# Four attention layers on one core: the key loads of every batch but the first moved from SyncE's queue to GpSimd's, on semaphores of their own

## The chip, the cores and the metric

The kernel runs on one core of a Trainium2 chip. Its time is the device time of one execution in microseconds, and the time of a kernel is the median of its runs. TensorE (PE in the profile) multiplies matrices, VectorE (DVE), ScalarE (ACT) and GpSimd (POOL) work elementwise, and SyncE (SP) here issues DMA transfers only. All five work at once and wait for one another through semaphores; each takes its own instructions in order.

## The reference

Four cross-attention layers act one after the other on x of 4 batches x 1024 tokens x 256 channels, all in float32. Layers 0 and 2 ("wide") have 16 heads of 64 and 154 keys from a context of 512 channels, and a bias of two masks on some key columns. Layers 1 and 3 ("narrow") have RMS-normed queries, 16 query heads of 16 on 4 key heads, and attend to the same context..

```python
def wide(h, ctx, mask_A, mask_B, Wq, Wk, Wv, Wo, bo, idx_A, idx_B):   # layers 0 and 2
    q, k, v = heads(h @ Wq), heads(ctx @ Wk), heads(ctx @ Wv)
    logits = einsum("bhqd,bhkd->bhqk", q, k) * 64 ** -0.5 + col_bias  # -20 (1 - mask) on idx_A, idx_B
    return einsum("bhqk,bhkd->bhqd", softmax(logits), v) @ Wo + bo + h
def narrow(x, cond, wq, wk, wv, wo, norm_w):                          # layers 1 and 3
    q = heads(rmsnorm(x, norm_w) @ wq)
    k, v = kv_heads(cond @ wk), kv_heads(cond @ wv)
    return x + softmax(q @ k.T / 4) @ v @ wo
```

## The kernel before

It has three parts. `prepare` (to about 200 us) splits the weights into a high and a low float32 half and writes keys and values of all batches and layers to DRAM scratch. `run_layers` does the layers. `store_outputs` transposes x back and stores it.

`run_layers` works through eight windows w (or `it`), two pairs of layers times four batches (w // 4 is the pair, w % 4 the batch). A window has four chunks of four steps: chunks 0 and 2 are the two token halves of the wide layer, chunks 1 and 3 those of the narrow one; chunk 1 in window w finishes the batch of window w - 1. A step n has a query projection ("query"), maxima of the scores ("max") that are turned and taken off ("turn"), scores of the last 26 keys ("rest") and of the first 128 ("score"), and the product with the values ("value"). Behind a chunk come the sums ("sums", "inverse"), the scaling of the kept results ("scale", on GpSimd), their high and low half ("norm" on ScalarE, "low" on VectorE) and the output projection ("output"). Ahead of a narrow chunk stand "squares", "square" and "rate", the norm of x.

The order is written out by hand in ORDER (lines 517 to 561), a list of entries such as "max 11 4" (step 11, part 4); "0+" is step 0 of the next window, "3-" one of the window before. Every engine walks this one list and does what is its own in each entry, so an entry's place is its place in each engine's in-order stream. `each_batch` (line 743) walks it for the four computing engines; SyncE walks it in `one_round` (line 905), and only there do "early", "nkeys" and "wkeys" have a meaning.

The keys of a window lie in single buffers in SBUF. "wkeys" has four parts: `load_wide_keys` issues 4 DMAs (w_top) and then 5, 5 and 5 (w_pair, w_rest, w_aux; w_val, w_val_rest), line 812. "nkeys" has four parts of 14, 13, 13 and 13 DMAs in `load_narrow_keys`, line 844; most have 16 partitions. The first part of each waits until TensorE's last value step on the old keys has been done ("value 7 1" and "value 11 1"). At window 4, where the second pair of layers begins, `load_key_rows` adds 8 DMAs and a wait for them; other loads of new weights (lines 768, 793, 802) also stand in SyncE's stream.

The places that matter in ORDER, one after the other: "value 8 0, nkeys 0 0, scale 0 3, ..., inverse 1, norm 0 3, nkeys 0 1, squares 3, square 3, rate 3, nkeys 0 2, nkeys 0 3, query 12 0, scale 1 0, scale 1 1, split 0+, wkeys 0+ 0, wkeys 0+ 1, scale 2 0, max 0+ 0, scale 2 1, wkeys 0+ 2, wkeys 0+ 3, scale 2 2, scale 2 3", and "rest 0" of the next window.

GpSimd (lines 1132 to 1150) has four kinds of work: the low half of the query input in "split" and "rate" (x_lo, line 1137), the reciprocal root in "square" (a power, line 1142) and two products in each "scale" (line 1149), which wait for inv_b. SyncE brings inv_b from DRAM in `spread_inverses` (line 903), a new one after each "scale" and the first after "inverse" (line 935). ScalarE copies x to x_hi in "rate" (line 1033) and the scaled results to a_hi in "norm" (line 1088). TensorE waits for the narrow keys in "query 12" (line 1264), for w_top in "max 0" and for the other wide keys in "rest 0" (line 1306); its query products are line 1273, the rate transposes line 1396, the rest step line 1316 and the output line 1382.

Of the kernel before, what the change touches and what calls it, by code (L numbers as in the profile page):

```python
# [14 lines left out]
F32 = mybir.dt.float32  # L15
# [640 lines left out]
def run_layers(nc, ins, dr):  # L656

    ctx = ExitStack()
    with ctx:
# [60 lines left out]
        wtops_loaded, wkeys_loaded, nkeys_loaded = sem("wtops_loaded"), sem("wkeys_loaded"), sem("nkeys_loaded")  # L720
        early_loaded = signal("early_loaded", "split", times=16)
# [21 lines left out]
        def each_batch(eng, do):  # L743

            for r in ROUNDS:
                for what, n, k, turn in WINDOW:
                    if what not in ("early", "nkeys", "wkeys") and present(r + turn, what, n):
                        do(r + turn, what, n, k)
# [13 lines left out]

        @block.sync
        def _(sp):
# [3 lines left out]

            def load_key_rows(p):  # L770

                for par in range(2):
                    a = 64 * (1 - par)
                    def every(buf):
                        return buf[a:a + 6].rearrange("p (h two) k -> p h two k", two=2)[:, :, par, :]
                    rows = dr["keyrows"][p]
                    sp.dma_start(every(w_aux), rows[:, None, 0:P].to_broadcast([6, 8, P])).then_inc(key_rows_loaded, 16)
                    sp.dma_start(every(w_top), rows[:, None, :].to_broadcast([6, 8, KEYS])).then_inc(key_rows_loaded, 16)
                for j in range(4):
                    a = 64 * (1 - j % 2)  # L780
                    rests = w_aux_rest[a:a + 6].rearrange("p (g j) k -> p g j k", j=4)
                    sp.dma_start(rests[:, :, j, 0:REST],
                                 dr["keyrows"][p][:, None, P:KEYS].to_broadcast([6, 4, REST])).then_inc(key_rows_loaded, 16)
# [19 lines left out]

            def cols(src, b):

                return src[..., bass.ds(b * P, P)], src[..., bass.ds(b * REST + B * P, REST)]

            def load_wide_keys(p, b, part):

                def go(dst, src, loaded=wkeys_loaded):
                    sp.dma_start(dst, src).then_inc(loaded, 16)

                def every(buf, par):
                    return buf.rearrange("p (h two) k -> p h two k", two=2)[:, :, par, :]

                if part == 0:
                    for par in range(2):
                        rows = slice(64 * par, 64 * par + 64)
                        main, rest = cols(dr["wk_hib"][p, rows], b)  # L820
                        go(every(w_top[rows], par)[:, :, 0:P], main, wtops_loaded)
                        go(every(w_top[rows], par)[:, :, P:KEYS], rest, wtops_loaded)
                elif part < 3:
                    par = part - 1
                    rows = slice(64 * par, 64 * par + 64)
                    main, _ = cols(dr["wk_hi"][p, rows], b)
                    rest = dr["wk_rest"][p, rows][..., bass.ds(b * REST, REST)]
                    for half in range(2):
                        to = slice(64 * half, 64 * half + 64)
                        go(every(w_pair[to], par).bitcast(F32), main)  # L830
                        go(every(w_rest[to], par)[:, :, 0:REST], rest)
                    main, _ = cols(dr["wk_lob"][p, rows], b)
                    go(every(w_aux[rows], par), main)
                else:
                    go(w_val[:], dr["wv"][p, bass.ds(b, 1)].rearrange("o p n -> p (o n)"))
                    for j in range(4):
                        dst = w_val_rest[32 * j:32 * j + REST].rearrange("p (g d) -> p g d", d=DW)
                        src = dr["wv_rest"][p, bass.ds(b * REST, REST)].rearrange("p (g j d) -> p g j d", j=4, d=DW)
                        go(dst, src[:, :, j, :])

            def load_narrow_keys(p, b, j):

                def go(dst, src):
                    sp.dma_start(dst, src).then_inc(nkeys_loaded, 16)

                def by_unit(src, w):
                    return src.rearrange("(u i) k -> i u k", i=DN)

                heads = lambda buf: buf.rearrange("p (u j) k -> p u j k", j=4)[:, :, j, :]
                main, rest = cols(dr["nk_hi"][p], b)  # L850
                for half in range(2):
                    to = slice(64 * half + DN * j, 64 * half + DN * j + DN)
                    go(heads(n_pair[to]).bitcast(F32), by_unit(main, P))
                    go(n_pair_rest[to, :, 32 * j:32 * j + REST].bitcast(F32), by_unit(rest, REST))
                lo, lo_rest = cols(dr["nk_lob"][p], b)
                hi, hi_rest = cols(dr["nk_hib"][p], b)
                for par in range(2):
                    to = slice(64 * par + DN * j, 64 * par + DN * j + DN)
                    odd = lambda ap: ap.rearrange("p (v two) k -> p v two k", two=2)[:, :, par, :]
                    go(odd(heads(n_aux[to])), odd(by_unit(lo, P)))  # L860
                    go(odd(n_aux_rest[to, :, 32 * j:32 * j + REST]), odd(by_unit(lo_rest, REST)))
                    go(odd(heads(n_top[to]))[:, :, 0:P], odd(by_unit(hi, P)))
                    go(odd(heads(n_top[to]))[:, :, P:KEYS], odd(by_unit(hi_rest, REST)))
                go(n_val_rest[32 * j:32 * j + REST], dr["nv_rest"][p, bass.ds(b * REST, REST)])
                if j == 0:
                    go(n_val[:], dr["nv"][p, bass.ds(b, 1)].rearrange("o p g d -> p (o g) d"))
# [38 lines left out]
            def one_round(r):  # L905

                for what, c, k, turn in WINDOW:
# [46 lines left out]
                    elif (what, c, k) == ("output", 2, 3) and w == B - 1:  # L954

                        wait(sp, pe_output.sem, pe_output.after(w, what, c, k))
                        wait(sp, dve_output.sem, dve_output.after(w, what, c, k))
                        load_wide_out(1)
                    elif (what, c, k) == ("query", 11, 1) and w == B - 1:

                        wait(sp, pe_query.sem, pe_query.after(w, what, c, k))
                        load_wide_query(1)
                    elif what == "early" and (w, c) != (0, 0):

                        before_w, before = back_chunk(w, c)
                        key = ("split" if before % 2 == 0 else "rate", before, 0)
                        wait(sp, act_split.sem, act_split.after(before_w, *key))
                        wait(sp, pool_split.sem, pool_split.after(before_w, *key))
                        if (w, c) == (B, 0):
                            sp.wait_ge(wide_query_loaded, 2 * WIDE_QUERY)  # L970
                        load_early(HALF[c], b)
                    elif what == "nkeys" and w > 0:

                        if k == 0:
                            wait(sp, pe_value.sem, pe_value.after(w, "value", 7, 1))
                            if w == B:
                                load_narrow_query(1)
                        if k == KVN - 1 and w == B:
                            sp.wait_ge(narrow_query_loaded, 2 * NARROW_QUERY)
                        load_narrow_keys(p, b, k)  # L980
                    elif what == "wkeys" and w > 0:

                        if k == 0:
                            wait(sp, pe_value.sem, pe_value.after(w - 1, "value", 11, 1))
                            if w == B:
                                load_key_rows(1)
                                sp.wait_ge(key_rows_loaded, 2 * KEY_ROWS)
                        load_wide_keys(p, b, k)
# [5 lines left out]
            load_wide_keys(0, 0, 0)  # L994
            load_key_rows(0)
            sp.wait_ge(cleared, CLEARED)
            for part in range(1, 4):
                load_wide_keys(0, 0, part)
# [5 lines left out]
            for part in range(KVN):  # L1004
                load_narrow_keys(0, 0, part)
# [89 lines left out]
        def _(pool):  # L1095
# [37 lines left out]
            def do(it, what, n, k):  # L1133
# [9 lines left out]
                elif what == "scale":  # L1143
# [6 lines left out]
                    last.then_inc(pool_scale.sem, 1)  # L1150

# [89 lines left out]
        def _(pe):  # L1241
# [19 lines left out]
            def do(it, what, n, k):  # L1261
                if what == "query":
                    if n == 3 * 4:
                        wait(pe, nkeys_loaded, (it + 1) * NKEYS)
# [10 lines left out]
                elif what == "max":  # L1275
                    if k == 0 or k == 4 and wide(n):
                        wait(pe, dve_aux.sem, dve_aux.after(it, *query_for(n, k // 4)))
                        if n == 0:
                            wait(pe, wtops_loaded, (it + 1) * WTOPS)
# [21 lines left out]
                elif what in ("rest", "score"):  # L1301
# [3 lines left out]
                    if (what, n) == ("rest", 0):  # L1305
                        wait(pe, wkeys_loaded, (it + 1) * WKEYS)
# [191 lines left out]
```

## Time and profile before

| | us |
|---|---|
| median of 3 runs | 1894.06 |
| lowest and highest | 1888.15, 1894.6 |
| the profiled execution | 1887.3 |
| its span, first to last instruction | 1885.2 |

| engine | busy us | share of the span | instructions |
|---|---|---|---|
| TensorE | 1707.6 | 91% | 10924 |
| VectorE | 1250.4 | 66% | 2393 |
| ScalarE | 1039.0 | 55% | 1761 |
| GpSimd | 428.5 | 23% | 299 |

A profile is of one execution and 2.1 us shorter in span than the execution's own time. A busy time is a sum over the instructions of an engine; a DMA issue counts for none, so SyncE has no row.
### The profile page before, as it was taken

The page shows a single profiled execution, that of the slowest core. Times are in us where ns is not written, and L with a number is a line of the kernel's source. Part 1 is how long each engine was busy: PE and PEld are TensorE (multiplying, and loading weights), DVE is VectorE, ACT ScalarE, POOL GpSimd, SP SyncE. Part 2 cuts the span into 40 slices and gives each one's busy share as a digit, 9 for nine tenths or more (in the row PEclk, how much of TensorE's full clock was granted, in tenths as well). Part 3 has the DMA queues.
Part 4 walks back from the last instruction along what each step waited for, and adds up shares of the span by engine and source line. Part 5 has one row for each costly group of instructions (what it writes and reads, how often), then busy time and mean ns, then how long its engine had stood idle before and what let it go on. Part 6 is the DMA issues. An engine that isn't in the chain of part 4 may idle for free. (4 is left out here: it accounts for less than half of the span.)

```text
span 1885.2 us, 29948 instructions
## 1 busy us (share of the span) xinstructions
PE 1707.6 (91%) x10924; PEld 938.6 (50%) x10924; DVE 1250.4 (66%) x2393; ACT 1039.0 (55%) x1761; POOL 428.5 (23%) x299
## 2 busy tenths in 40 slices
PE   6897596989999999999899999899999999999564
PEld 5786343444545454545445454445454545454333
DVE  4447554667867686778567777577777777776432
ACT  1111063666666666666556666566666666666231
POOL 4242302121212121212111312131313121312201
PEclk9998688999999999999999999899999999999786
DMA  7986541051216131612242324222322333222105
GB/s 272 310 274 213 128 127 47 13 101 35 75 44 124 35 73 46 124 36 74 89 95 86 82 52 99 57 71 59 83 65 71 60 82 66 70 60 60 47 25 200
DMA packets 173272, 175.78 MB, mean 93 GB/s; under 512 B 89345, under 2 KB 129661, under 8 KB 171016
## 3 DMA queue, kind: packets, MB, share of 16 engines
q1 hardware_dynamic: 170824, 163.39, 33.1%
q10 hardware_dynamic: 2304, 10.49, 1.4%
q8 instruction: 88, 1.44, 0.3%
q14 instruction: 56, 0.46, 0.1%
HBM read 127.17 MB, written 46.63 MB: 92 GB/s over the span
## 5 line engine op out<-in xcount | busy, mean ns | idle before, releaser
L1189 DVE TENSOR_REDUCE tops<-general 128x2 bf16<-128x308 f32 x1024 | 436.5, 472 | 107.1 <-PE general L1292 48.6
L1149 POOL TENSOR_TENSOR kept<-kept,inv_b 128x512 f32<-128x512 f32 x192 | 258.5, 1367 | 650.5 <-DMA inv_b<-scratch_inverses 650.5
L1052 ACT ACTIVATE probs<-score_ps 128x512 f32<-128x512 f32 x512 | 299.1, 597 | 139.1 <-PE score_ps L1328 131.9
L1176 DVE CAST q_aux<-q_pair 64x512 bf16<-64x512 f32 x160 | 78.1, 488 | 208.2 <-ACT q_pair L1040 207.4
L1062 ACT ACTIVATE q_aux<-general 4x512 bf16<-4x512 bf16 x320 | 187.3, 585 | 13.7 <-PE general L1299 6.9
L1039 ACT ACTIVATE q_pair<-general 64x512 fp32r<-64x512 f32 x160 | 94.5, 591 | 178.4 <-PE general L1273 178.2
L1088 ACT ACTIVATE a_hi<-kept 128x512 fp32r<-128x512 f32 x192 | 109.9, 621 | 121.9 <-PE general L1382 66.5
L1202 DVE TENSOR_TENSOR a_lo<-kept,a_hi 128x512 fp32r<-128x512 f32 x192 | 157.0, 858 | 28.6 <-ACT a_hi L1088 27.5
L1222 DVE TENSOR_TENSOR x<-general,x 128x512 f32<-128x512 f32 x160 | 108.6, 690 | 80.8 <-PE general L1382 79.5
L1288 PE MATMUL general<-w_top,q_aux 128*128 128x154 bf16 x1024 | 125.9, 234 | 23.9 <-DVE q_pair L1179 10.8
L1137 POOL TENSOR_TENSOR x_lo<-xn,x_hi 128x1024 fp32r<-128x1024 f32 x32 | 75.8, 2368 | 311.9 <-ACT x_hi L1020 161.0
L1343 PE MATMUL out_ps<-probs,w_val 128*64 128x512 f32 x512 | 137.0, 619 | 0.7 <-ACT probs L1052 0.7
L1074 ACT ACTIVATE kept<-out_ps 128x512 f32<-128x512 f32 x192 | 104.2, 595 | 57.3 <-PE sum_ps L1357 42.2
L1292 PE MATMUL general<-n_top,q_aux 128*128 128x308 bf16 x512 | 129.3, 300 | 6.5 <-DVE q_aux L1177 2.8
L1327 PE MATMUL score_ps<-q_pair,n_pair 128*128 128x512 f32 x256 | 125.1, 497 | 8.8 <-ACT probs L1052 7.3
L1273 PE MATMUL general<-x_hi,wq_hi 128*128 128x512 f32 x256 | 115.5, 451 | 19.0 <-POOL x_lo L1137 18.6
L1288 PEld LDWEIGHTS general<-w_top,q_aux 128*128 128x128 bf16 x1024 | 79.3, 99 | 102.6 <-issue 37.5
L1382 PE MATMUL general<-a_hi,wo_hi 128*128 128x512 f32 x256 | 113.2, 442 | 13.7 <-DVE q_pair L1179 5.9
L1327 PE MATMUL score_ps<-q_pair,w_pair 128*128 128x512 f32 x256 | 122.2, 482 | 0.8
L1178 DVE TENSOR_TENSOR q_pair<-general,q_pair 64x512 fp32r<-64x512 f32 x160 | 109.5, 684 | 5.0
L1179 DVE TENSOR_TENSOR q_pair<-general,q_pair 64x512 fp32r<-64x512 f32 x160 | 111.0, 693 | 2.2
L1052 ACT ACTIVATE probs_rest<-score_ps 128x512 f32<-128x512 f32 x128 | 76.2, 595 | 54.9 <-PE score_ps L1328 38.1
(150 smaller groups left out, 3252.0 us busy)
## 6 DMA issues: line engine op xcount, KB each, us to landing
inv_b<-scratch_inverses SPq DMA_DIRECT2D x128, 256.0 KB
inv_b<-scratch_inverses SPq DMA_DIRECT2D x128, 128.0 KB
xn<-scratch_stream SPq DMA_DIRECT2D x16, 512.0 KB, 4.1
w_pair<-scratch_wk_hi SPq DMA_DIRECT2D x32, 256.0 KB
x<-scratch_stream SPq DMA_DIRECT2D x16, 512.0 KB, 3.4
scratch_stream<-x SPq DMA_DIRECT2D x16, 512.0 KB, 3.9
scratch_wk_hi<-p_kout_hi SPq DMA_DIRECT2D x16, 308.0 KB
p_raw<-in_L_xattn_Wk_dram SPq DMA_DIRECT2D x4, 1024.0 KB, 8.2
```

The lines of the kernel that those rows point to most:

```text
L1052: nc.scalar.activation(dst, score_ps[:, number % 2, :], ACT.Exp, scale=scale).then_inc(act_exp.sem, 1)
L1062: last = nc.scalar.activation(q_aux[a:a + 4, half_of(n), slot(n), j, :], ps[0:4].bitcast(BF16)[:, 0:TOK], ACT.Copy, scale=-1.0)
L1149: last = nc.gpsimd.tensor_tensor(tile, tile, inv_b[:, i, :], ALU.mult)
L1179: last = nc.vector.tensor_tensor(q_pair[0:64, s, j + 1, :], ps[64:P], q_pair[64:P, s, j + 1, :], ALU.subtract)
L1189: last = nc.vector.tensor_reduce(tops[:, n % 2, sub, 2 * pair:2 * pair + 2], src, AX_X, ALU.max)
L1202: last = nc.vector.tensor_tensor(a_lo[:, i, :], kept[:, place(tile), :], a_hi[:, i, :], ALU.subtract)
L1273: last = nc.tensor.matmul(ps, l, r, start=(i == 0), stop=(i == len(pairs) - 1))
L1288: last = nc.tensor.matmul(ps[:, i * KEYS:(i + 1) * KEYS], q[:, 2 * pair + i, sub], w_top[:, 4 * (n % 4) + 2 * pair + i, :], start=True, st ...
L1292: last = nc.tensor.matmul(ps[:, 0:2 * KEYS], q[:, n % 2, sub], n_top[:, h:h + 2, :].rearrange("p h k -> p (h k)"), start=True, stop=True)
L1327: nc.tensor.matmul(ps, keys[0], q_pair[:, s, unit, :], start=True, stop=False)
L1343: last = nc.tensor.matmul(out_ps[64 * i:64 * i + 64, k, :], w_val[:, h * DW:(h + 1) * DW], probs[:, 2 * k + i, :], start=True, stop=False, ...
L1382: last = nc.tensor.matmul(ps, l, r, start=(i == 0), stop=(i == len(pairs) - 1))
```

## The change

SyncE keeps the keys of window 0. Those of windows 1 to 7, narrow and wide, and the key rows of the second pair are issued by GpSimd, at the same entries of ORDER. The three loading functions move out of SyncE's block to the scope around it and take the engine and the semaphore as arguments; what they move is unchanged. Four new semaphores count GpSimd's loads, and TensorE waits on them from window 1 on. `each_batch` now passes "nkeys" and "wkeys" on; the other computing engines have no branch for them. The two waits on "value" go along to GpSimd, and SyncE keeps the one ahead of its narrow query weights at window 4.

```diff
@@ semaphores @@
+        wtops_again, wkeys_again, nkeys_again = sem("wtops_again"), sem("wkeys_again"), sem("nkeys_again")
+        key_rows_again = sem("key_rows_again")
@@ each_batch @@
-                    if what not in ("early", "nkeys", "wkeys") and present(r + turn, what, n):
+                    if what != "early" and present(r + turn, what, n):
@@ the loads, now outside SyncE's block @@
+        def load_key_rows(eng, p, loaded):
...
+        def load_wide_keys(eng, p, b, part, loaded, tops):
+            def go(dst, src, loaded=loaded):
+                eng.dma_start(dst, src).then_inc(loaded, 16)
...
+        def load_narrow_keys(eng, p, b, j, loaded):
+            def go(dst, src):
+                eng.dma_start(dst, src).then_inc(loaded, 16)
...
@@ SyncE, one_round @@
-                        if k == 0:
+                        if k == 0 and w == B:
                             wait(sp, pe_value.sem, pe_value.after(w, "value", 7, 1))
-                            if w == B:
-                                load_narrow_query(1)
+                            load_narrow_query(1)
                         if k == KVN - 1 and w == B:
                             sp.wait_ge(narrow_query_loaded, 2 * NARROW_QUERY)
-                        load_narrow_keys(p, b, k)
-                    elif what == "wkeys" and w > 0:
-
-                        if k == 0:
-                            wait(sp, pe_value.sem, pe_value.after(w - 1, "value", 11, 1))
-                            if w == B:
-                                load_key_rows(1)
-                                sp.wait_ge(key_rows_loaded, 2 * KEY_ROWS)
-                        load_wide_keys(p, b, k)
@@ GpSimd @@
+                elif what == "nkeys" and it > 0:
+
+                    if k == 0:
+                        wait(pool, pe_value.sem, pe_value.after(it, "value", 7, 1))
+                    load_narrow_keys(pool, it // B, it % B, k, nkeys_again)
+                elif what == "wkeys" and it > 0:
+
+                    if k == 0:
+                        wait(pool, pe_value.sem, pe_value.after(it - 1, "value", 11, 1))
+                        if it == B:
+                            load_key_rows(pool, 1, key_rows_again)
+                            pool.wait_ge(key_rows_again, KEY_ROWS)
+                    load_wide_keys(pool, it // B, it % B, k, wkeys_again, wtops_again)
@@ TensorE @@
-                        wait(pe, nkeys_loaded, (it + 1) * NKEYS)
+                        wait(pe, nkeys_loaded if it == 0 else nkeys_again, max(it, 1) * NKEYS)
...
-                            wait(pe, wtops_loaded, (it + 1) * WTOPS)
+                            wait(pe, wtops_loaded if it == 0 else wtops_again, max(it, 1) * WTOPS)
...
-                        wait(pe, wkeys_loaded, (it + 1) * WKEYS)
+                        wait(pe, wkeys_loaded if it == 0 else wkeys_again, max(it, 1) * WKEYS)
```

## Rows read from the trace of the kernel before

**Rows 1.** The page, first part: TensorE's busy time, share of the span, instructions.

```profile
PE 1707.6 (91%) x10924; PEld 938.6 (50%) x10924; DVE 1250.4 (66%) x2393; ACT 1039.0 (55%) x1761; POOL 428.5 (23%) x299
```

**Rows 2.** Windows from query 12 to query 12: length, busy time by engine, clock, DMA.

```profile
549.00:738.00 189.00, 185.66 (x1249) 95.91 (x1248) 141.03 (x267) 125.24 (x217) 43.20 (x31) 1.00 0.30 70
738.00:932.00 194.00, 186.25 (x1250) 95.91 (x1250) 141.63 (x267) 126.59 (x218) 46.68 (x33) 1.00 0.32 78
932.00:1127.00 195.00, 189.92 (x1247) 98.21 (x1248) 139.45 (x266) 124.39 (x215) 40.50 (x28) 0.97 0.32 81
1127.00:1324.00 197.00, 187.00 (x1249) 96.26 (x1248) 139.95 (x267) 125.08 (x216) 43.47 (x31) 0.97 0.31 69
```

**Rows 3.** Waits of TensorE, 300 to 1760 us: who for whom, total us, times, longest.

```profile
PE score_ps L1316 <- issue: 9.7, 2, 9.0
PE score_ps L1327 <- ACT probs L1052: 7.1, 4, 3.9
...
PE general L1273 <- DMA n_val_rest<-scratch_nv_rest: 5.8, 1, 5.8
```

**Rows 4.** Timeline of SyncE's queue: start us, us, engine line op, [idle before]; narrow keys.

```profile
509.57 0.34 SPq L844 DMA_DIRECT2D n_pair<-scratch_nk_hi  x1
...
539.66 0.43 SPq L844 DMA_DIRECT2D n_pair_rest<-scratch_nk_hi  x1
540.13 0.43 SPq L844 DMA_DIRECT2D n_pair<-scratch_nk_hi  x1
...
930.43 0.40 SPq L844 DMA_DIRECT2D n_val_rest<-scratch_nv_rest  x1
```

**Rows 5.** Timeline of GpSimd, windows 1 and the turn to 2.

```profile
546.88 2.36 POOL L1137 TENSOR_TENSOR x_lo<-xn,x_hi 128x1024 fp32r<-128x1024 f32 x1 [8.65 <-ACT x_hi L1033]
549.21 2.52 POOL L1149 TENSOR_TENSOR kept<-kept,inv_b 128x512 f32<-128x512 f32 x2
...
581.92 2.59 POOL L1149 TENSOR_TENSOR kept<-kept,inv_b 128x512 f32<-128x512 f32 x2 [14.50 <-DMA inv_b<-scratch_inverses]
590.26 2.51 POOL L1149 TENSOR_TENSOR kept<-kept,inv_b 128x512 f32<-128x512 f32 x2 [5.74 <-DMA inv_b<-scratch_inverses]
```

**Rows 6.** Timeline of TensorE: rate transposes, query 12, first rest step, query 12 of window 3.

```profile
543.24 0.65 PE L1396 MATMUL general<-ident,rate 128*128 128x128 f32 x4
...
549.35 0.47 PE L1273 MATMUL general<-x_hi,nq_hi 128*128 128x512 f32 x1
...
608.48 1.06 PE L1316 MATMUL score_ps<-q_pair,w_rest 128*32 128x512 f32 x8 [0.74 <-issue]
...
932.18 0.80 PE L1273 MATMUL general<-x_hi,nq_hi 128*128 128x512 f32 x1 [5.77 <-DMA n_val_rest<-scratch_nv_rest]
```

**Rows 7.** GpSimd's groups of instructions, shapes apart: operation, shapes, count, busy us, mean ns.

```profile
L1142 POOL TENSOR_TENSOR rate<-meansq,power 128x4 f32<-128x4 f32 x16 | 16.1, 1009 | 308.2 <-DVE meansq L1226 308.2
...
L1117 POOL TENSOR_SCALAR_AFFINE_SELECT w_aux<-w_aux 4x512 bf16<-4x512 bf16 x4 | 2.5, 632 | 0.6 <-POOL x_lo L1137 0.2
...
L1488 POOL MEMSET const-float32-0.0<- 128x1 f32 x1 | 0.1, 99 | 0.2 <-issue 0.2
```

**Rows 8.** Windows of 2 us behind TensorE's longest wait, columns as in rows 2.

```profile
1192.00:1194.00 2.00, 1.16 (x8) 0.44 (x12) 1.49 (x3) 0.00 (x0) 0.00 (x0) 0.50 0.73 160
1194.00:1196.00 2.00, 2.00 (x11) 0.56 (x3) 0.00 (x0) 0.60 (x1) 0.00 (x0) 0.50 0.61 119
1196.00:1198.00 2.00, 2.00 (x9) 1.60 (x9) 0.08 (x1) 0.60 (x1) 1.99 (x2) 0.92 0.07 16
```

**Rows 9.** Timeline of ScalarE: the copies that read "scale 0 3" and "scale 2 2".

```profile
525.79 1.15 ACT L1088 ACTIVATE a_hi<-kept 128x512 fp32r<-128x512 f32 x2 [1.73 <-PE general L1382]
...
606.23 1.15 ACT L1088 ACTIVATE a_hi<-kept 128x512 fp32r<-128x512 f32 x2 [2.37 <-PE general L1382]
```

**Rows 10.** Timeline of SyncE's queue: one wide key load.

```profile
577.58 0.63 SPq L812 DMA_DIRECT2D w_rest<-scratch_wk_rest  x1
```

**Rows 11.** VectorE's casts into q_aux, whole run: duration ns min/median/max, first and last start.

```profile
L1176 DVE CAST q_aux<-q_pair x160: 408/420/1547, 223.0 to 1795.9; 64x512 bf16<-64x512 f32 x160
```

More of the change, by code:

```diff
@@ L761, in bank_of, with every @@
             return general[:, BANK[use], :]
+        def load_key_rows(eng, p, loaded):
+            for par in range(2):
+                a = 64 * (1 - par)
+                def every(buf):
+                    return buf[a:a + 6].rearrange("p (h two) k -> p h two k", two=2)[:, :, par, :]
+                rows = dr["keyrows"][p]
+                eng.dma_start(every(w_aux), rows[:, None, 0:P].to_broadcast([6, 8, P])).then_inc(loaded, 16)
+                eng.dma_start(every(w_top), rows[:, None, :].to_broadcast([6, 8, KEYS])).then_inc(loaded, 16)
+            for j in range(4):
+                a = 64 * (1 - j % 2)
+                rests = w_aux_rest[a:a + 6].rearrange("p (g j) k -> p g j k", j=4)
+                eng.dma_start(rests[:, :, j, 0:REST],
+                             dr["keyrows"][p][:, None, P:KEYS].to_broadcast([6, 4, REST])).then_inc(loaded, 16)
@@ new lines, in cols, with every @@
+        def cols(src, b):
+            return src[..., bass.ds(b * P, P)], src[..., bass.ds(b * REST + B * P, REST)]
+        def load_wide_keys(eng, p, b, part, loaded, tops):
+            def go(dst, src, loaded=loaded):
+                eng.dma_start(dst, src).then_inc(loaded, 16)
+            def every(buf, par):
+                return buf.rearrange("p (h two) k -> p h two k", two=2)[:, :, par, :]
+            if part == 0:
+                for par in range(2):
+                    rows = slice(64 * par, 64 * par + 64)
+                    main, rest = cols(dr["wk_hib"][p, rows], b)
+                    go(every(w_top[rows], par)[:, :, 0:P], main, tops)
+                    go(every(w_top[rows], par)[:, :, P:KEYS], rest, tops)
+            elif part < 3:
+                par = part - 1
+                rows = slice(64 * par, 64 * par + 64)
+                main, _ = cols(dr["wk_hi"][p, rows], b)
+                rest = dr["wk_rest"][p, rows][..., bass.ds(b * REST, REST)]
+                for half in range(2):
+                    to = slice(64 * half, 64 * half + 64)
+                    go(every(w_pair[to], par).bitcast(F32), main)
+                    go(every(w_rest[to], par)[:, :, 0:REST], rest)
+                main, _ = cols(dr["wk_lob"][p, rows], b)
+                go(every(w_aux[rows], par), main)
+            else:
+                go(w_val[:], dr["wv"][p, bass.ds(b, 1)].rearrange("o p n -> p (o n)"))
+                for j in range(4):
+                    dst = w_val_rest[32 * j:32 * j + REST].rearrange("p (g d) -> p g d", d=DW)
+                    src = dr["wv_rest"][p, bass.ds(b * REST, REST)].rearrange("p (g j d) -> p g j d", j=4, d=DW)
+                    go(dst, src[:, :, j, :])
@@ new lines, in load_narrow_keys, with by_unit @@
+        def load_narrow_keys(eng, p, b, j, loaded):
+            def go(dst, src):
+                eng.dma_start(dst, src).then_inc(loaded, 16)
+            def by_unit(src, w):
+                return src.rearrange("(u i) k -> i u k", i=DN)
+            heads = lambda buf: buf.rearrange("p (u j) k -> p u j k", j=4)[:, :, j, :]
+            main, rest = cols(dr["nk_hi"][p], b)
+            for half in range(2):
+                to = slice(64 * half + DN * j, 64 * half + DN * j + DN)
+                go(heads(n_pair[to]).bitcast(F32), by_unit(main, P))
+                go(n_pair_rest[to, :, 32 * j:32 * j + REST].bitcast(F32), by_unit(rest, REST))
+            lo, lo_rest = cols(dr["nk_lob"][p], b)
+            hi, hi_rest = cols(dr["nk_hib"][p], b)
+            for par in range(2):
+                to = slice(64 * par + DN * j, 64 * par + DN * j + DN)
+                odd = lambda ap: ap.rearrange("p (v two) k -> p v two k", two=2)[:, :, par, :]
+                go(odd(heads(n_aux[to])), odd(by_unit(lo, P)))
+                go(odd(n_aux_rest[to, :, 32 * j:32 * j + REST]), odd(by_unit(lo_rest, REST)))
+                go(odd(heads(n_top[to]))[:, :, 0:P], odd(by_unit(hi, P)))
+                go(odd(heads(n_top[to]))[:, :, P:KEYS], odd(by_unit(hi_rest, REST)))
+            go(n_val_rest[32 * j:32 * j + REST], dr["nv_rest"][p, bass.ds(b * REST, REST)])
+            if j == 0:
+                go(n_val[:], dr["nv"][p, bass.ds(b, 1)].rearrange("o p g d -> p (o g) d"))
@@ L768, in load_wide_query @@
                     sp.dma_start(wq[i][:].bitcast(F32), dr["wq_" + a][p]).then_inc(wide_query_loaded, 16)
[L770 to L783, printed above, removed]
             def load_wide_out(p):
@@ L802, in load_narrow_out @@
                             sp.dma_start(dst[:, :, v, :].bitcast(F32), src[v, j]).then_inc(narrow_out_loaded, 16)
[L804 to L866, printed above, removed]
@@ L993, in _ @@
             load_masks()
[L994 to L995 removed]
+            load_wide_keys(sp, 0, 0, 0, wkeys_loaded, wtops_loaded)
+            load_key_rows(sp, 0, key_rows_loaded)
             sp.wait_ge(cleared, CLEARED)
             for part in range(1, 4):
[L998 removed]
+                load_wide_keys(sp, 0, 0, part, wkeys_loaded, wtops_loaded)
             load_wide_out(0)
@@ L1004, in _ @@
             for part in range(KVN):
-                load_narrow_keys(0, 0, part)
+                load_narrow_keys(sp, 0, 0, part, nkeys_loaded)
             sp.wait_ge(wide_out_loaded, WIDE_OUT)
```

## The prediction

> **What bounds the kernel now.** The page comes first: TensorE is busy 91% of the span, and in its second part TensorE's line is nines and a few eights from the ninth slice to the last three, so the layers are bound by TensorE and everything else works in its shadow [rows 1]. The windows cut at the start of the third narrow query (query 12) come next: an undisturbed stage of one batch takes 189 us (the first row stands for three such), three take 194, 195 and 197 [rows 2]. So the time that the layers lose beyond their own rhythm is 5 + 6 + 8 = 19 us in all. The list of what TensorE waited for between 300 and 1760 us gives two causes that have to do with keys: 5.8 us for the last narrow key load, once, and 9.7 us ahead of the first rest step, nearly all of it one wait of 9.0 us [rows 3]. Those two waits are the most that a faster supply of keys could take away, and the reader should hold on to that: a change of who issues the keys has little to win.
>
> What it can lose is read from SyncE's own timeline. SyncE issues a narrow key load every 0.47 us (539.66, 540.13), and in window 1 it starts as early as 509.57 [rows 4]. GpSimd's timeline of the same stretch shows the work among which the loads are to stand [rows 5], and TensorE's the two moments that matter: the rate transposes at 543.24 and query 12 at 549.35, with no idle time noted for either [rows 6].
>
> **The change, part by part.** SyncE loses 72 issues per batch: 53 narrow (14 + 13 + 13 + 13) and 19 wide (4 + 5 + 5 + 5). The same 72 go into GpSimd's in-order stream, at the places that ORDER gives them, for seven batches. The two waits per batch on TensorE's value steps, the eight key-row loads and a wait for their landing go along. TensorE's own waits change their semaphore, not their number; I cost that at nothing, as each waits for the same data. No byte more is moved.
>
> Let t be GpSimd's time for one narrow issue. No row of this trace shows a DMA issued by GpSimd, so t is bounded. From below: SyncE's pitch of 0.47 us [rows 4]; GpSimd's cheapest operation, a fill of one column, takes 0.10 us, but that one writes nothing but a constant [rows 7]. From above: 1.6 us, the power operation (1.01 us) and the small diagonal fill (0.63 us) one after the other [rows 7]. I take t = 1.0 us. The nearest row is the power operation on four columns: it has next to no data, so its 1.01 us is a routine's fixed cost, and a DMA issue is again a routine with next to no data of its own. The rest is worked out at 1.0, and repeated at the ends.
>
> *Narrow keys, parts 2 and 3 (26 loads).* Here is the step that decides. In ORDER they stand behind "rate 3" and ahead of "query 12". On SyncE that was harmless, since SyncE does nothing in "rate". On GpSimd "rate 3" is the subtraction x_lo, which waits 8.65 us for ScalarE and ends at 546.88 + 2.36 = 549.24 [rows 5]. Query 12 starts at 549.35, 0.1 us later [rows 6], and the same pair of times, 0.1 us apart, recurs in all other windows but the one with the wait. So the 26 loads can't begin before the very moment at which TensorE wants them landed. The landing takes 1.75 us from the last issue: SyncE's last load of window 3 starts at 930.43, TensorE goes on at 932.18 [rows 4, 6]. The new wait is 26 x 1.0 + 1.75 - 0.10 = 27.65 us per batch. Nothing hides it: TensorE is in order, and value 10, the rest step and the maxima of chunk 3 stand behind query 12. Behind the loads on GpSimd stands "scale 1 0", which began at once at 549.21 and now runs 26 us later, that is beside the same wait, so it adds nothing; the next late thing after the wait is TensorE alone.
>
> *What a wait costs beyond itself.* After the 9.0 us wait the granted clock shows 0.50 in 1192 to 1196 and 0.92 in the next 2 us: that is 1.2 of 2.4 GHz for 1.16 + 2.00 us of matmul work, and a little of 2 us more [rows 8]. Lost: (1.16 + 2.00) / 2 + 0.16 = 1.7 us. A wait of 28 us lets the clock fall all the same. So 27.65 + 1.7 = 29.4 us, times seven: 205.5 us.
>
> *Narrow keys, parts 0 and 1 (27 loads).* They may start at 509.5, when the value step that frees the buffers has ended (SyncE's first one started at 509.57 [rows 4]). 14 loads end at 523.5, "scale 0 3" (2.5 us) at 526.0; ScalarE starts the copy that reads it at 525.79 [rows 9], so 0.2 us late. 13 more loads end at 539.0, the power operation at 540.0; TensorE's rate transposes start at 543.24 [rows 6]. Cost nothing at t = 1.0, with TensorE's 3.2 us of slack as cover. The cover is gone at 27 t + 2.5 + 1.0 = 33.7, so t = 1.12; beyond that each 0.1 us costs 2.7 us per batch (4.9 us at t = 1.3, 13 us at 1.6).
>
> *Wide keys.* A wide issue keeps SyncE for 0.63 us, a narrow one for 0.43, with 0.04 between two [rows 4, 10]: a factor 0.67 / 0.47 = 1.4, which I carry over: 1.4 us each. Parts 0 and 1, nine loads, 12.6 us, lie in the 14.5 us in which GpSimd waits ahead of 581.92 [rows 5]: hidden. Parts 2 and 3, ten loads, begin when "scale 2 1" ends at 592.8 and end at 606.8 in place of a free 7.2 us; "scale 2 2" then ends at 609.3, and ScalarE wants it at 606.23 [rows 5, 9]: 3.1 us late. ScalarE is in order too, and the exponentials of the next scores stand behind that copy, so I count all of it: times seven, 21.5 us. The keys themselves land at about 608.5, when the rest step wants them at 608.48 [rows 6].
>
> *Once, at window 4.* Eight key-row loads and their landing, 8 x 1.0 + 1.75, come ahead of the nine wide ones: 22.4 us against 14.5. 7.9 us late, where 3.9 us of waiting already lies in that stage of 195 us [rows 2, 3]: plus 4 us.
>
> *What is won.* In window 3 the keys stood behind two loads of query weights, and the 5.8 us with its low clock (1.7 us) is part of the new wait now: 7.5 us. In window 4 the 16 loads of narrow output weights no longer hold up the last wide keys, but they still hold up inv_b, which goes out behind them: I count 1.5 us of the 9.0. The 36 us per batch that SyncE no longer spends on issues buy no more, since inv_b is on time in the 189 us stages.
>
> The Trainium skill speaks against the move in two places. "SBUF — State Buffer", Who interferes with whom, says that VectorE in a two-port mode and GpSimd block each other for a whole instruction, and that descriptors of a GpSimd DMA wait for it. The trace agrees that something holds them up: VectorE's casts take 0.42 us and up to 1.55 [rows 11]. Four pairs of casts lie between 509 and 540, 3.4 us, just above the slack of 3.2; by that the sum would be 7 x 0.2 = 1.4 us more, and nothing in the stretch of 26 loads, where VectorE has run dry. "DMA: Bandwidth & Descriptors", Latency and other measured facts, puts the first byte of a DMA from GpSimd at about 1 us against 0.6; by that the landing would be 0.4 us later, 2.8 us in all. No run here shows it.
>
> **Sum.** 205.5 + 21.5 + 4 - 7.5 - 1.5 = 222 us on top of the profiled execution's 1887.3 us, which is 2109 us. That execution is 6.8 us under the median of the runs, 1894.06, and about equal to the fastest; put on the median, 2116, and I say 2115 us.
>
> **The rivals.**
> *Cheap issues (0.22).* GpSimd issues at SyncE's pace, t = 0.47, wide ones at 0.65. Then the wait is 12.2 + 1.65 = 13.9 us, with the clock 15.6, times seven 109; all else is hidden, window 4 gets its 3.9 us back too, and 13 us are won: about 1990 us. For it speaks that the loads are small (16 partitions); against it that SyncE's issues are done by a queue that does nothing else. At t = 0.7 it is 2035.
> *Dear issues (0.22).* t = 1.3, wide ones 1.8: the wait is 35.5 us, with the clock 37.2; narrow parts 0 and 1 add 4.9, the wide ones 7.1; times seven 344; with the rest (10 more at window 4, 9 won) 2240 us. At 1.6 us it is 2385. For it speaks that the wide loads have 512 rows each, and that something must write these down; against it that SyncE's price rises by 1.4 only.
> *Faster than before (0.03).* GpSimd hands its DMAs over without being held up, a tenth of a microsecond each as for its cheapest operation, and the 19 us of the disturbed stages come back. But even so 26 x 0.1 + 1.65 = 4.3 us per batch is waited, 30 us in all. The sign turns where the wait is under 19 / 7 = 2.7 us, so at t = 0.04 us, or where the loads run ahead of x_lo. It would then be about 1870 us. Against it stands the order: the wait for ScalarE stands in the same stream ahead of them.
> *No effect (0.03).* GpSimd's stream isn't in order for DMAs and the loads land in time as before: 1890 us.
>
> **How the numbers follow.** My forecast, t from 0.85 to 1.15, has 0.50: 2070 to 2165 us. The likeliest time is its middle. For eight times in ten the range takes in most of the cheap and of the dear case: 2015 (t = 0.6) to 2250 us (t a little over 1.3). A measurement of this kernel can tell 0.5%, some 9 us. Slower by more than that: 0.50 + 0.22 + 0.22 = 0.94, and 0.01 of what is left; faster 0.02; the same 0.03.
>
> **What would show it.** In the profile after, seven waits of TensorE at query 12, for a DMA that fills narrow keys, of some 28 us each; stages of about 220 us; GpSimd's 26 issues back to back from the end of x_lo; no 5.8 us apart in window 3. If these waits are there with another length, t was wrong and nothing else. If x_lo or the power operation comes late, parts 0 and 1 are dearer than I think. The prediction is wrong in kind if the loads start before x_lo has ended, or if TensorE's waits stand at the scales and not at the query.

## The result

| | before | after |
|---|---|---|
| median, us | 1892.6 | 1994.22 |
| lowest and highest | 1888.15, 1894.6 | 1993.7, 1995.69 |
| the profiled execution | 1887.3 | 1993.7 |
| its span | 1885.2 | 1991.6 |

The kernel before has one run more here than when the forecast was made. The change makes the kernel slower: the ratio is 1.0545, 95% interval 1.0526 to 1.0564. By the two medians that is 101.6 us, by the two profiled executions 106.4 us. The forecast was 2115 us, with a range from 2015 to 2250 us: the kernel is slower, as forecast, but by 102 us and not by some 220.

The page of the kernel after, its first line and the two queues that carry the work (packets, MB, share of 16 engines' time):

```profile
PE 1721.1 (86%) x10924; PEld 943.9 (47%) x10924; DVE 1248.5 (63%) x2393; ACT 1038.5 (52%) x1761; POOL 710.4 (36%) x811
...
q1 hardware_dynamic: 92648, 141.87, 25.2%
q0 software_dynamic: 18960, 21.53, 6.0%
```

TensorE has the same 10924 instructions in a longer span; that they take 1721.1 us in place of 1707.6 [rows 1] is put down to slow clock further down (e2). A queue that was not there before, q0, has taken over 21.5 MB. GpSimd's busy time is 710.4 us against 428.5: unlike an issue of SyncE, a DMA issue of GpSimd does count as busy, so what is said of issues beside the table of the kernel before holds for SyncE alone.

The windows of the kernel after, cut at query 12, with columns as in [rows 2]:

```profile
567.00:771.00 204.00, 187.46 (x1248) 96.88 (x1248) 139.19 (x266) 125.36 (x216) 82.69 (x103) 0.97 0.27 64
771.00:976.00 205.00, 187.79 (x1248) 96.89 (x1248) 140.48 (x266) 125.35 (x216) 83.72 (x103) 0.97 0.30 74
976.00:1181.00 205.00, 188.11 (x1248) 96.70 (x1248) 143.89 (x266) 125.47 (x216) 89.27 (x111) 0.97 0.31 77
1181.00:1389.00 208.00, 190.34 (x1248) 98.58 (x1248) 139.85 (x266) 125.12 (x216) 77.79 (x95) 0.96 0.28 65
```

Each stage takes 204 to 208 us where an undisturbed one took 189. The busy times of all engines but GpSimd are those of before within about 2%. What TensorE waited for between 300 and 1860 us (total, times, longest):

```profile
PE general L1278 <- DMA n_val_rest<-scratch_nv_rest: 99.2, 7, 14.4
...
PE general L1387 <- DVE a_lo L1207: 4.8, 2, 4.6
PE score_ps L1332 <- ACT probs L1044: 4.8, 4, 4.3
...
PE score_ps L1321 <- issue: 3.9, 3, 1.8
```

The first line is nearly the whole result. It stands for seven waits, 99.2 us in all and 14.2 on average, where before there was one of 5.8 us [rows 3]. The line of the rest step, 9.7 us with one wait of 9.0 there, is down to 3.9 us. GpSimd's timeline of window 1:

```profile
513.64 0.59 POOL L821 DMA_DIRECT2D n_pair<-scratch_nk_hi  x1 [3.13 <-PE out_ps L1374]
...
520.88 3.03 POOL L1141 TENSOR_TENSOR kept<-kept,inv_b 128x512 f32<-128x512 f32 x2
...
541.05 1.03 POOL L1134 TENSOR_TENSOR rate<-meansq,power 128x4 f32<-128x4 f32 x1 [10.61 <-DVE meansq L1231]
550.70 2.37 POOL L1129 TENSOR_TENSOR x_lo<-xn,x_hi 128x1024 fp32r<-128x1024 f32 x1 [8.62 <-ACT x_hi L1025]
553.01 0.56 POOL L821 DMA_DIRECT2D n_pair<-scratch_nk_hi  x1
...
565.57 0.53 POOL L821 DMA_DIRECT2D n_val_rest<-scratch_nv_rest  x1
566.11 2.50 POOL L1141 TENSOR_TENSOR kept<-kept,inv_b 128x512 f32<-128x512 f32 x2
...
613.54 0.71 POOL L789 DMA_DIRECT2D w_pair<-scratch_wk_hi  x1
```

and TensorE's:

```profile
547.06 0.65 PE L1401 MATMUL general<-ident,rate 128*128 128x128 f32 x4
...
567.45 0.79 PE L1278 MATMUL general<-x_hi,nq_hi 128*128 128x512 f32 x1 [14.14 <-DMA n_val_rest<-scratch_nv_rest]
```

x_lo ends at 550.70 + 2.37 = 553.07. The first of the 26 issues starts at 553.01 and the last at 565.57, and "scale 1 0" comes behind them. TensorE goes on at 567.45, after 14.14 us of waiting. The length of an issue is in GpSimd's groups, shapes apart (count, busy us, mean ns):

```profile
L821 POOL DMA_DIRECT2D n_aux_rest<-scratch_nk_lob x56 | 28.5, 508 | 0.0
...
L789 POOL DMA_DIRECT2D w_rest<-scratch_wk_rest x28 | 19.1, 682 | 0.0
...
L789 POOL DMA_DIRECT2D w_val<-scratch_wv x7 | 4.1, 582 | 0.0
```

A narrow issue takes 0.508 us, a wide one with 512 rows 0.682, and w_val's, with few long rows, 0.582.

### The profile page after: what moved, and what is told of

The parts are those of the page before. It is cut to its first block and busy times, and to the rows that moved or that the text cites. A ratio compares the mean times of both kernels' runs of the same rounds, so it can differ in the third digit from the quotient of the medians.

```text
span 1991.6 us, 29949 instructions
## 1 busy us (share of the span) xinstructions
PE 1721.1 (86%) x10924; PEld 943.9 (47%) x10924; DVE 1248.5 (63%) x2393; ACT 1038.5 (52%) x1761; POOL 710.4 (36%) x811
## 3 DMA queue, kind: packets, MB, share of 16 engines
q1 hardware_dynamic: 92648, 141.87, 25.2%
q0 software_dynamic: 18960, 21.53, 6.0%
## 5 line engine op out<-in xcount | busy, mean ns | idle before, releaser
L1278 PE MATMUL general<-x_hi,nq_hi 128*128 128x512 f32 x64 | 33.2, 519 | 104.1 <-DMA n_val_rest<-scratch_nv_rest 99.2
```

The lines of the kernel that those rows point to most:

```text
L1278: last = nc.tensor.matmul(ps, l, r, start=(i == 0), stop=(i == len(pairs) - 1))
```

## The experiments

Two theories were open after the comparison. By the first, the loss is made by the place of the narrow parts 2 and 3 in GpSimd's stream, behind x_lo, and by nothing else. By the second, loads from GpSimd are dearer wherever they stand. Four smaller questions were open too: what a wait costs beyond its length, whether the wide loads cost anything, what VectorE does to GpSimd's issues, and where a gain is to be had.

**The two parts ahead of x_lo (e1).** The kernel after, with two entries of ORDER moved:

```diff
-        max 10 3, score 9 3, max 10 4, value 9 0, max 10 5, max 10 6, square 3, max 10 7, query 11 0,
+        max 10 3, score 9 3, max 10 4, value 9 0, max 10 5, nkeys 0 2, max 10 6, square 3, max 10 7, nkeys 0 3, query 11 0,
         query 11 1, turn 10, value 9 1, rate 3, max 11 0, max 11 1,
-    rest 10, max 11 2, score 10 0, max 11 3, nkeys 0 2, max 11 4, max 11 5, score 10 1, nkeys 0 3,
+    rest 10, max 11 2, score 10 0, max 11 3, max 11 4, max 11 5, score 10 1,
```

> The changed kernel with two entries of ORDER moved: narrow part 2 stands ahead of 'square 3', part 3 ahead of 'rate 3', so all 53 narrow issues on GpSimd are over before x_lo. Theory (the place in GpSimd's stream decides): the seven waits of 14.2 us at query 12 go, with about 1.7 us of low clock each: 1994 - 7 x 15.9 = 1883 us, a few us under the kernel before. Rival (loads from GpSimd are costly wherever they stand: slow landings, late scales): the waits shrink but 20 us or more of the loss stay, 1912 us or above.

Measured: 1880.12 us, ratio to before 0.9938 (0.992 to 0.9956). GpSimd's timeline in window 1, and under it TensorE's query 12:

```profile
534.61 0.53 POOL L821 DMA_DIRECT2D n_val_rest<-scratch_nv_rest  x1
539.21 1.03 POOL L1134 TENSOR_TENSOR rate<-meansq,power 128x4 f32<-128x4 f32 x1 [4.06 <-DVE meansq L1231]
...
546.27 0.54 POOL L821 DMA_DIRECT2D n_val_rest<-scratch_nv_rest  x1
548.96 2.36 POOL L1129 TENSOR_TENSOR x_lo<-xn,x_hi 128x1024 fp32r<-128x1024 f32 x1 [2.15 <-ACT x_hi L1025]
551.28 2.52 POOL L1141 TENSOR_TENSOR kept<-kept,inv_b 128x512 f32<-128x512 f32 x2
```

```profile
551.42 0.47 PE L1278 MATMUL general<-x_hi,nq_hi 128*128 128x512 f32 x1
```

Part 2 ends at 535.1, ahead of the power operation; part 3 lies between 540.20 and 546.81, in time that GpSimd otherwise spends waiting for x_hi; 2.15 us of that wait are left. x_lo ends at 551.32 and query 12 starts at 551.42 with no idle time. All seven waits at query 12 are gone, and the time is under that of the kernel before, with the same 72 loads on the same engine. So the second theory falls as the cause of the loss; a small price of the wide loads comes out below (e3).

**The same move with all keys on SyncE (e5).** The kernel before, with the same edit of ORDER.

> The kernel before, all keys on SyncE, with the same two entries moved. Theory: only the 5.8 us wait of window 3 goes, because the narrow keys now stand ahead of the wide query weights in SyncE's queue; with its low clock 7 us, so 1885 us; the 9.0 us wait of window 4 stays. Rival (the order has no part, the gain of the other kernel is GpSimd's): 1892 us. If the order alone does as well as the order with GpSimd, GpSimd brings nothing.

Measured: 1879.67 us, ratio 0.9939 (0.9917 to 0.996). TensorE's waits there:

```profile
PE score_ps L1316 <- issue: 8.9, 1, 8.9
...
PE score_ps L1327 <- ACT probs L1052: 6.6, 6, 3.1
```

The wait of 5.8 us in window 3 is gone. The one of 8.9 us stays; it stands at the first rest step of window 5, behind the loads of window 4. SyncE alone with the order does as well as GpSimd with the order. I had expected 1885 us, 7 us less than before; the interval is 7.6 to 15.7 us, and what makes up the rest is not shown.

**Wide keys alone on GpSimd (e3).** Narrow keys go back to SyncE:

```diff
+                        load_narrow_keys(sp, p, b, k, nkeys_loaded)
...
-                    if what != "early" and present(r + turn, what, n):
+                    if what not in ("early", "nkeys") and present(r + turn, what, n):
...
-                        wait(pe, nkeys_loaded if it == 0 else nkeys_again, max(it, 1) * NKEYS)
+                        wait(pe, nkeys_loaded, (it + 1) * NKEYS)
```

> Wide keys and key rows on GpSimd, narrow keys back on SyncE. Theory: no wait at query 12 but the one of window 3 (5.8 us); 19 issues of 0.7 us lie in GpSimd's idle time, window 4's wait of 9.0 us shrinks to about 5: 1885 to 1892 us. Rival (wide issues make the scales late): 3 us and more per batch, 1912 us or above.

Measured: 1889.38 us, ratio 0.9994 (0.9979 to 1.0009). GpSimd's timeline around the wide loads of window 1:

```profile
575.87 0.68 POOL L789 DMA_DIRECT2D w_aux<-scratch_wk_lob  x1
586.67 2.53 POOL L1143 TENSOR_TENSOR kept<-kept,inv_b 128x512 f32<-128x512 f32 x2 [10.12 <-DMA inv_b<-scratch_inverses]
...
601.93 2.38 POOL L789 DMA_DIRECT2D w_val_rest<-scratch_wv_rest  x4
605.08 2.97 POOL L1143 TENSOR_TENSOR kept<-kept,inv_b 128x512 f32<-128x512 f32 x2 [0.76 <-DMA inv_b<-scratch_inverses]
```

Nine of them end at 576.55, 10 us ahead of "scale 2 0". The other ten end at 604.3, and "scale 2 2" starts at 605.08, still with 0.76 us of idle time for inv_b. It is the same in all seven windows: both scales that stand behind wide loads wait for inv_b. So the wide loads hold up no scale, and in sum they cost nothing that can be measured. Of the 9.0 us at the first rest step of window 5, 1.6 are left, with 4.8 us for a_lo behind them.

They are not free, though. SyncE writes the sums of a chunk to DRAM and reads them back (scratch_sums, spread_sums), and VectorE's reciprocal waits for them. On SyncE the first four wide loads (w_top) stood behind that round trip; on GpSimd they go out as soon as x_lo has ended, beside it. The kernel before:

```profile
567.77 0.53 SPq L916 DMA_DIRECT2D scratch_sums<-wide_sums  x1
569.63 0.34 SPq L925 DMA_DIRECT2D spread_sums<-scratch_sums  x1
570.02 2.58 SPq L812 DMA_DIRECT2D w_top<-scratch_wk_hib  x4
571.49 0.55 DVE L1196 RECIPROCAL inv<-spread_sums 128x64 f32<-128x64 f32 x1
```

and e3:

```profile
570.36 2.83 POOL L789 DMA_DIRECT2D w_top<-scratch_wk_hib  x4
570.77 0.53 SPq L918 DMA_DIRECT2D scratch_sums<-wide_sums  x1
573.65 0.34 SPq L927 DMA_DIRECT2D spread_sums<-scratch_sums  x1
578.86 0.55 DVE L1203 RECIPROCAL inv<-spread_sums 128x64 f32<-128x64 f32 x1 [4.50 <-DMA spread_sums<-scratch_sums]
```

From the first issue to the reciprocal it takes 8.1 us, where it took at most 3.7 before. Six windows of e3 have such a wait of VectorE, of 3.0 to 4.5 us, and so have e1 and the kernel after (1.4 to 4.5 us); in before, e4, e5 and e8, with the wide keys on SyncE, none at that place is longer than 0.3 us. TensorE pays for part of it: from query 12 of window 0 to query 4 of window 1 it needs 97.3 to 97.8 us in the six kernels with wide keys on GpSimd, and 93.0 to 95.7 in the four others. So about 2 us are lost there, 1 to 5 us in the next window (99.2 us in e1, 99.4 in e3 and 96.8 in e7, against 95.6 before and 94.7 in e5), and none that can be seen in later ones. That eats up most of the 6.5 us that the wide keys bring at windows 4 and 5 (below). e3 beside e4 shows that the wide loads on GpSimd do it; that it is the moment of w_top, and what its data and the sums share, is not shown, as no run moves w_top alone.

**Narrow keys alone on GpSimd (e4).** This is the mirror image: wide keys and key rows go back to SyncE.

> Narrow keys on GpSimd, wide ones back on SyncE. Theory: the seven waits of 14.2 us stay, and the 9.0 us wait of window 4 comes back in part: 1994 to 2000 us. Rival (the loss is shared by the wide loads): clearly under 1990 us.

Measured: 2001.28 us, ratio 1.0583 (1.0557 to 1.0609).

```profile
PE general L1285 <- DMA n_val_rest<-scratch_nv_rest: 102.2, 7, 17.4
PE score_ps L1328 <- issue: 8.4, 2, 7.8
```

The time is 1.3 us above the range expected. The seven waits carry all of the loss. One of them is 17.4 us long, with a gap of 3.05 us between GpSimd's issues for which the trace names no cause, and the wait at the first rest step of window 5 is back (7.8 us).

**Half of the issues behind x_lo (e2).** As e1, but part 3 stays where it was, at "rest 10":

> The changed kernel with narrow part 2 moved ahead of 'square 3' and part 3 left where it was, so 13 issues in place of 26 lie between x_lo and query 12. If a wait is (issues x 0.505) + 1.65 us of landing, it is now 8.2 us, seven times. If the low clock behind a wait costs 1.7 us whatever the wait's length: 1880 + 7 x (8.2 + 1.7) = 1949 us. If what a wait costs beyond itself grows with its length (half as much here): 1943 us. If a fixed price per wait outweighs the issues (a landing of 5 us or more): above 1965 us.

Measured: 1947.68 us, ratio 1.0318 (1.0294 to 1.0341).

```profile
PE general L1278 <- DMA n_val_rest<-scratch_nv_rest: 53.5, 7, 7.7
```

These are seven waits of 7.6 us. 13 issues fewer save 45.7 us of waiting in all, so 6.5 per wait and 0.50 us per issue, which is the length of an issue; a line through the two points leaves 1.1 us that doesn't depend on the number.

Against e1 the time is 67.6 us longer and the waits are 53.5, so each costs 2.0 us beyond its length; for the kernel after, 114.1 and 99.2, it is 2.1. The three were not timed together; with the ratios to the kernel before of each comparison the two numbers are 2.6 and 2.2. TensorE's busy time gives the same without any such comparison: e1 has 1704.8 us, e2 1721.9 and the kernel after 1721.1, for the same instructions, so 2.4 and 2.3 us more per wait. It is a price per wait, and not one that grows with the microseconds waited. Most of it is seen in the windows around the wait of window 1 of the kernel after (TensorE's busy time first, the granted clock third from the end):

```profile
554.00:566.00 12.00, 0.00 (x0) 0.00 (x0) 0.00 (x0) 0.00 (x0) 12.00 (x25) 0.64 0.18 21
566.00:568.00 2.00, 0.55 (x1) 0.50 (x2) 0.00 (x0) 0.00 (x0) 1.98 (x3) 0.50 0.05 8
568.00:570.00 2.00, 2.00 (x6) 1.32 (x4) 0.00 (x0) 0.00 (x0) 0.61 (x1) 0.50 0.09 29
570.00:572.00 2.00, 2.00 (x11) 0.83 (x12) 0.36 (x1) 1.55 (x3) 0.00 (x0) 0.76 0.71 191
572.00:574.00 2.00, 2.00 (x24) 0.36 (x32) 1.86 (x4) 1.97 (x4) 0.51 (x1) 1.00 0.91 238
```

The clock has gone to 1.2 of 2.4 GHz during the wait; it stays there for 2.55 us of work and for half of the next 2 us: 0.55 / 2 + 2.00 / 2 + 0.24 x 2.00 = 1.75 us. The same sum behind the wait of 7.7 us in e2 (0.50 in 561 to 563, 0.67 in 563 to 565) gives 1.6. Where the other half microsecond goes is not shown.

**Copies on VectorE beside the 26 issues (e6).** The kernel after, and in VectorE's part of query 12, ahead of its wait:

```diff
+                    if n == 12 and it > 0:
+                        for i in range(36):
+                            made = 36 * (it - 1) + i
+                            wait(dve, copied, made - 2)
+                            nc.vector.tensor_copy(idle_out[:, made % 3], idle_in[:]).then_inc(copied, 1)
```

> The changed kernel plus 36 VectorE copies of a constant tile (float32, 128 x 512) ahead of VectorE's part in query 12 of windows 1 to 7, that is beside GpSimd's 26 issues, while VectorE has nothing else to do. If copies and GpSimd's descriptor writing shut each other out, the 26 issues stretch from 13.1 us to 20 us or more and the time is 1994 + 7 x 7 = 2043 us or above. If they don't meet, an issue keeps its 0.505 us, the copies end inside the wait, and the time is 1994 to 2000 us.

Measured: 2014.47 us, ratio 1.067 (1.0648 to 1.0692). GpSimd's issues, VectorE's copies in the same stretch, and TensorE's waits:

```profile
553.15 0.68 POOL L823 DMA_DIRECT2D n_aux<-scratch_nk_lob  x1
...
561.21 0.68 POOL L823 DMA_DIRECT2D n_pair_rest<-scratch_nk_hi  x1
...
562.54 0.51 POOL L823 DMA_DIRECT2D n_aux_rest<-scratch_nk_lob  x1
...
564.53 0.50 POOL L823 DMA_DIRECT2D n_aux_rest<-scratch_nk_lob  x1
```

```profile
550.22 12.23 DVE L1185 COPY idle_out<-idle_in 128x512 f32<-128x512 f32 x36
```

```profile
PE general L1286 <- DMA n_val_rest<-scratch_nv_rest: 120.5, 7, 17.3
```

While the copies run, to 562.45, an issue takes 0.67 or 0.68 us (the first 0.78); from 562.54 on it is 0.51 again. 36 copies in 12.23 us are 0.34 each, so an issue takes the time of just two copies, and each ends 0.1 us behind the end of a copy. The copies keep their pace. The seven waits are 17.2 us on average, against 14.2. That is 21.3 us in all, and the time grew by 20.2 (24 by the ratios). The trace agrees with the rule of the Trainium skill that the prediction weighed ("SBUF — State Buffer", Who interferes with whom), in that GpSimd is held until an instruction of VectorE has ended. But neither of the two expectations has the size: with copies as short as these the issue is held up by 0.17 us, and is not shut out for the whole run of 36.

**The output weights later (e7 and e8).** At window 4 SyncE loads 16 pieces of narrow output weights ahead of the last inv_b. e7 is e1 and e8 is e5, both with those loads behind it:

```diff
                         wait(sp, pool_scale.sem, pool_scale.after(w, what, c, k))
                         spread_inverses(c, k + 1)
+                        if (w, c, k) == (B, 2, 2):
+                            wait(sp, pe_output.sem, pe_output.after(w, "output", 1, 1))
+                            load_narrow_out(1)
                     elif (what, c, k) == ("output", 1, 1):
...
-                        if w == B:
-                            wait(sp, pe_output.sem, pe_output.after(w, what, c, k))
-                            load_narrow_out(1)
```

> e1 (keys on GpSimd, narrow parts 2 and 3 ahead of x_lo) and, once, at window 4, SyncE's 16 loads of narrow output weights moved from ahead of the last inv_b loads of chunk 2 to behind them. Theory: the 4.6 us wait for a_lo that e1 still has there goes, with its low clock: 1880 - 6 = 1874 us. Rival (the wait comes from elsewhere, or turns up behind the later loads): 1880 us.

> The reordered kernel with all keys on SyncE (e5) and the same move of the 16 output weight loads. Theory: the 8.9 us wait at the first rest step of window 5 goes, since the last wide keys no longer stand behind them: 1880 - 10 = 1870 us, level with GpSimd's version or a little under it, so that GpSimd's part of the gain is nothing. Rival (SyncE needs the relief by GpSimd): 3 us or more above GpSimd's version.

Measured: e7 1872.97 us, ratio 0.9924 (0.9904 to 0.9944); e8 1872.29 us, ratio 0.9918 (0.9901 to 0.9934). The wait of 4.6 us for a_lo that e1 has in window 5 is gone in e7, and the 8.9 us at the rest step of e5 in e8. Both beat the kernel before by under 1%, and they are level. With the order mended, it makes no difference that can be measured who issues the keys. How much of the gain is that of the later loads is less sure: by medians it is 7 us against e1 and e5, which were timed in another comparison; by the ratios to the kernel before it is 3 to 4 us, and the intervals overlap.

## Why the prediction was right and where it was wrong

- **The step that decides was right.** The 26 loads can't begin before x_lo has ended, and query 12 is due 0.1 us later: all seven waits stand at query 12, for a narrow load, with the issues back to back from the end of x_lo and "scale 1 0" behind them at no cost. e1 and e2 show that the place alone does it.
- **The term that was mis-sized is t.** It was put at 1.0 us by the power operation of [rows 7]; it is 0.51. The reason given, that a DMA issue is "again a routine", was an analogy and no measurement. SyncE's pitch of 0.47 us [rows 4], the lower bound, was the row of the same instruction with the same shapes, and it was off by 0.04. The forecast was 121 us too high. Of these 26 x 0.49 x 7 = 89 are t at query 12, 21.5 the wide keys and 7.9 window 4, which both hang on t as well. The cheap rival, built on SyncE's pitch, came to about 1990 us and the kernel to 1994.22; it had a chance of 0.22.
- **The range was wrong too, as it stopped at t = 0.6 inside its own bounds.** It was closed on the side where the nearest row stood.
- **The landing was right but for a slip in the sum.** The 1.75 us run from the start of SyncE's last issue, 0.40 us long, so 26 t + 1.75 counts the last issue twice. From its end the landing is 932.18 - 930.83 = 1.35 us on SyncE, and 567.45 - 566.10 = 1.35 on GpSimd. The wait starts 0.24 us behind the end of x_lo and 0.30 behind the first issue: 26 x 0.505 + 1.35 - 0.30 = 14.2 us, as measured, where the recorded sum gives 14.9 at t = 0.51. Data that GpSimd asked for land no later than SyncE's.
- **The clock was near.** It was put at 1.7 us per wait; 2.0 to 2.6 were measured, and the windows show 1.75 of it.
- **The wide keys were put at 21.5 us for late scales, and no scale is late (e3).** The factor of 1.4 held (0.682 / 0.508 = 1.34); with the right t ten loads take 6.6 us and end ahead of inv_b. What they do cost, the late sums of windows 0 and 1, was not in the prediction, which looked at GpSimd's stream and not at what else is being moved when its loads go out. The parts 0 and 1 of the narrow keys cost nothing, as forecast, and the power operation ends 5.0 us ahead of the rate transposes (542.08 against 547.06), as it did before.
- **Window 4.** Plus 4 us was forecast for the key rows. In place of that the eight of them, their landing and nine wide loads end at 1008.34 on GpSimd, 0.69 us before inv_b comes, and the wait of 3.9 us that stood there is gone. (The 4.3 us for an exponential in the list above are another one, in window 0 at 400.35; it was 2.8 us before.) The 5.8 us of window 3 are part of the new wait, as forecast. At the first rest step of window 5, 9.0 us became 1.8, but 4.6 us for a_lo came behind it: 2.6 us are won in place of 1.5.
- **Put together:** 99.2 us of waits and 7 x 2.1 us of clock are 113.9; less 5.8 + 1.7, 2.6 and 3.9, plus 1.5 in window 0, that is 101.4 us. The medians differ by 101.6 us, the profiled executions by 106.4. That it fits so closely is in part by construction, since the 2.1 us come from the medians themselves; with the 1.75 us of the windows it is 99 us.
- **What VectorE does to the issues** was put at 1.4 us, since its casts are few there. e6 shows the mechanism when it is forced; in the kernel after, the narrow issues of window 1 take 0.50 to 0.59 us throughout, and no cost of it can be seen.

## What to carry to other kernels

When work moves to another in-order engine, don't ask first what it costs there but what it now stands behind: here 26 cheap issues cost 14 us of waiting and 2 us of clock a batch because they had come to stand behind an operation that is due when they are. Ask next what now leaves at the same moment: the wide loads had stood behind the sums and came to go out beside them. An instruction that the trace doesn't show was priced better here by the same instruction on another engine (off by 0.04 us) than by another instruction on the same engine (off by 0.5); keep the nearest bound in the range in any case. And when a queue has taken over too much, look at the order within it: moving two entries won as much here with the old queue as with the new one.

## What the runs showed of the hardware

- A DMA issue on GpSimd is short here and rises little with its rows: 0.51 us for 32 or 64 rows, 0.58 for w_val, 0.68 for 512. On SyncE the same loads took 0.43 and 0.63 us [rows 4, 10].
- The same 21.5 MB need 18960 packets when GpSimd issues them; SyncE's queue lost 170824 - 92648 = 78176. The time of all packets hardly changed: 33.1% of a span of 1885.2 us are 624 us of 16 engines, 25.2 + 6.0% of 1991.6 are 621.
- A load's data landed 1.35 us behind the end of its issue, from SyncE's queue and from GpSimd's alike.
- A wait of TensorE cost 2.0 to 2.6 us on top of its length, 1.6 to 1.75 of it seen in the clock behind it, whether it was 7.6 or 14.2 us long.
- With wide loads going out from GpSimd beside it, the sums' way to DRAM and back took 8.1 us, where it took at most 3.7 before (e3, window 1).
- Copies on VectorE that follow without a gap stretch a GpSimd issue from 0.51 to 0.68 us, two copies of 0.34.
